# Expert weights of a mixture-of-experts layer: when they are loaded, in which order, and where their halves lie

## The reference

```
x = x + tanh(g_xattn) * xattn(layernorm(x), ctx, seg_id, Wq, Wkv, Wo)   # 16 heads, each token sees 4 context rows
x = x + tanh(g_ffn) * ffn(layernorm(x), gate_w, w1, b1, w2, b2)
# ffn: gate_probs = softmax(x @ gate_w.T); comb_w = the two largest probabilities, 0 elsewhere
for e in range(8):
    h = silu(x @ w1[e] + b1[e])            # w1[e]: 256 x 1024
    out = out + (h @ w2[e] + b2[e]) * comb_w[..., e]   # w2[e]: 1024 x 256
```

## Time and profile before

| | us |
|---|---|
| median of 3 runs (lowest, highest) | 345.33 (344.28, 345.51) |
| the profiled execution, device time | 344.77 |
| its span | 342.9 |
| PE busy | 312.0 (91%) |
| DVE busy | 250.8 (73%) |
| ACT busy | 189.5 (55%) |
| POOL busy | 198.6 (58%) |
| moved by DMA | 58.96 MB, 28.22 of them on q1 and 26.63 on q0 |

### The profile page before, as it was taken

The page is one execution under the profiler, slowest core; times in us unless marked ns, Lnnn a source line. Parts: engine busy times, 40 slices in busy tenths (PEclk is TensorE's granted clock), DMA queues, the critical chain, the costliest instruction groups (busy, mean ns, idle before and its releaser), DMA issues.

```text
span 342.9 us, 11216 instructions
## 1 busy us (share of the span) xinstructions
PE 312.0 (91%) x3305; PEld 253.4 (74%) x3305; DVE 250.8 (73%) x593; ACT 189.5 (55%) x526; POOL 198.6 (58%) x223
## 2 busy tenths in 40 slices
PE   7798989999998869999999999999999998999920
PEld 6457878888898658788878887878878776778710
DVE  4759999999998957868877688786886865464610
ACT  2451355665475358666767667667676655455410
POOL 2456889887764053346666666676676655663330
PEclk9899999999999999999999999999999999999985
DMA  7799999999899746245453553544545455453320
GB/s 249 235 341 417 403 419 404 414 405 387 292 381 383 259 105 161 39 76 77 67 95 56 89 88 60 93 66 79 85 68 86 79 66 95 54 94 45 35 22 10
DMA packets 51097, 58.96 MB, mean 172 GB/s; under 512 B 24424, under 2 KB 45120, under 8 KB 48864
## 3 DMA queue, kind: packets, MB, share of 16 engines
q0 software_dynamic: 9408, 26.63, 31.7%
q1 hardware_dynamic: 36320, 28.22, 26.8%
q10 hardware_dynamic: 5312, 3.37, 3.2%
HBM read 43.32 MB, written 10.16 MB: 156 GB/s over the span
## 4 chain that ended last, share of the span: by engine, by line
PE 64%; DVE 21%; issue 5%; ACT 3%; DMA 2%; POOL 2%; ACTq 0%; DVEq 0%; SPq 0%; POOLq 0%
PE ps L1143 29%; PE ps L1157 16%; PE ps L1158 8%; DVE ps L1312 5%; DVE sel L1308 2%; PE ps L1163 2%; DVE w_parts L1308 2%; PE ps L920 2%; DMA w_parts<-in_L_xattn_Wkv 2%; DVE xs L1344 1%; PE ps L1162 1%; PE ps L979 1%; DVE rden L1331 1%; DVE ps L1316 1%; PE ps L988 1%
## 5 line engine op out<-in xcount | busy, mean ns | idle before, releaser
L1143 PEld LDWEIGHTS ps<-sel,w_parts 128*128 x1776 | 120.9, 98 | 35.9 <-issue 4.0
L1143 PE MATMUL ps<-sel,w_parts 128*128 128x128 f16 x1776 | 142.1, 219 | 2.2 <-ACT sel L847 1.0
L627 POOL DMA_INDIRECT out<-sel x37 | 59.2, 1601 | 80.0 <-ACT sel L855 62.9
L869 ACT ACTIVATE sel<-ps,b1T 128x128 f32<-128x128 f32 x296 | 83.4, 368 | 29.7 <-PE ps L1143 26.2
L1157 PE MATMUL ps<-w_parts,sel 128*128 x259 | 96.0, 379 | 0.4 <-issue 0.3
L1158 PE MATMUL ps<-w_parts,sel 128*128 x259 | 70.6, 273 | 0.0
L1535 DVE SCALAR_TENSOR_TENSOR w_parts<-w_parts (+1 forms) x32 | 39.2, 1230 | 32.1 <-ACT w_parts L838 19.9
L619 POOL DMA_INDIRECT sel<-tokens_split,sel x37 | 45.1, 1219 | 16.9 <-DVE sel L1517 10.3
L1550 DVE SCALAR_TENSOR_TENSOR sel<-sel 128x512 f16<-128x512 f32 x74 | 51.2, 692 | 2.5
L1548 DVE TENSOR_SCALAR sel<-sel 128x512 f16<-128x512 f32 x74 | 31.9, 432 | 16.5 <-ACT sel L869 16.2
L855 ACT ACTIVATE sel<-xn,sel 128x256 f32<-128x256 f32 x37 | 18.8, 509 | 37.8 <-DVE xn L1590 34.1
(11 more groups left out here) (223 smaller groups left out, 423.2 us busy)
## 6 DMA issues: line engine op xcount, KB each, us to landing
w_parts<-in_L_ffn_w SPq DMA_DIRECT2D x16, 1024.0 KB
out<-xs SPq DMA_DIRECT2D x16, 128.0 KB
tokens_split<-xsplit ACTq DMA_DIRECT2D x13, 128.0 KB, 6.0
xs<-in_x ACTq DMA_DIRECT2D x2, 512.0 KB, 7.2
xs<-in_x SPq DMA_DIRECT2D x2, 512.0 KB, 6.9
near_rows<-w_parts SPq DMA_DIRECT2D x4, 256.0 KB, 6.2
xs<-in_L_ffn_b SPq DMA_DIRECT2D x1, 1024.0 KB
sel<-tokens_split,sel POOLq DMA_INDIRECT x37
```

Of the source, the lines that this page charges most:

```text
L627: pool.indirect_dma_start(out_rows, bass.IndirectOffsetOnAxis(slot_row[:, at(q - 1)], 0), y_sb[(k + 3) % 4], None, compute_op=ALU.add).the ...
L869: act.activation(h32[n][:, c * P:c * P + P], ps_h[n][:, c * P:c * P + P], ACT.Silu, bias=biases[:, c:c + 1], scale=1.0 / (X_SCALE * W_SCALE))\
L1143: mm = pe.matmul(ps_h[n][:, c * P:c * P + P], w, xx, start=(i == 0), stop=(i == len(products) - 1))
```

## The change

The expert weights are no longer loaded during attention. The ranks are sent through PE (a column of ranks), ACT, POOL (a one-hot matrix), PE (the expert of each rank) and ACT to POOL, which writes them as integers into `order_i`. SP then issues the first two weight DMAs (expert of rank 0) with a row offset from a register; two more come behind the DMA transpose of tile 1, and each further one behind the transpose of an even tile. Weight DMA t is now that of rank t//2. With that the splits have constant places: raw place u+2 to place u. ACT waits for each DMA by its own semaphore, in front of the split that reads it. PE reads one number for each tile, its rank, and none for tile 0. The computation of `tile_p` in the first steps and three DVE operations in front of the list (`order_i` from `r_rank`) are gone.

```diff
-        def weights_in(eng, t):
-
-            e, k = t // 2, t % 2
+        def weights_in(eng, e, t):
+
+            k = t % 2
             rows = (w1_rows, w2_rows)[k]
             n = (D, F)[k]
             dst = w_parts[:, 2 * t + 2:2 * t + 4, :, :].rearrange("p u a c -> p (u a c)").bitcast(F32)\
                 .rearrange("p (k n) -> p k n", k=n // P)
-            eng.dma_start(dst, rows[e * n:e * n + n, :].rearrange("(k p) n -> p k n", p=P)).then_inc(s[f"w_in{k}"], 16)
+            eng.dma_start(dst, rows[bass.ds(e * n, n), :].rearrange("(k p) n -> p k n", p=P)).then_inc(s[f"w_in{t}"], 16)
...
-                now, added = tiles_in(t, 0, -2)
-                if now and t % 2 == 0 and t < 14:
-                    sp.wait_ge(s["kprod"], t + 1)
-                    weights_in(sp, t // 2)
-                if t == T + 1:
-                    sp.wait_ge(s["aT_ps"], T)
-                    weights_in(sp, 10)
+                added, = tiles_in(t, -2)
                 if added:
                     sp.wait_ge(s["x1_ok"], t - 1)
                     sp.dma_start(out_v[t - 2], xs[:, t - 2, :]).then_inc(s["out_in"], 16)
-                if t == 13:
-                    for b in range(B):
-                        sp.wait_ge(s[f"kv_out{b}"], 16)
-                    sp.wait_ge(s["wT_ok"], 2)
-                    sp.wait_ge(s["sel_in7"], 32)
-                    for u in range(11, T):
-                        weights_in(sp, u)
-                if 14 <= t <= T:
-                    sp.wait_ge(s["aT_ps"], t - 1)
-                    weights_in(sp, t - 7)
...
             sp.dma_start(xd_comb[:, SEEN:T, :], r_comb[:, SEEN:T, :]).then_inc(s["comb_in"], 16)
+            for b in range(B):
+                sp.wait_ge(s[f"kv_out{b}"], 16)
+            sp.wait_ge(s["wT_ok"], 2)
+            sp.wait_ge(s["aT_ps"], T)
+            sp.wait_ge(s["order_ok"], 1)
+            ranked = [None] * E
+
+            def weights_of(t):
+
+                if t % 2 == 0:
+                    ranked[t // 2] = sp.value_load(order_i[0:1, t // 2:t // 2 + 1], min_val=0, max_val=E - 1)
+                weights_in(sp, ranked[t // 2], t)
+
+            weights_of(0)
+            weights_of(1)
...
             tokens_turned(1)
+            weights_of(2)
+            weights_of(3)
...
             for q in range(2, NT):
                 tokens_turned(q)
+                if q % 2 == 0 and q // 2 + 3 < 2 * E:
+                    weights_of(q // 2 + 3)
...
+            pool.wait_ge(s["rank_ok"], 1)
+            pool.tensor_scalar(rank_hot[:, :], iota[0:E, 0:E], rank_col[:, 0:1], None, ALU.is_equal).then_inc(s["rank_hot_ok"], 1)
+            pool.wait_ge(s["order_f_ok"], 1)
+            pool.tensor_copy(order_i[:, :], order_f[:, :]).then_inc(s["order_ok"], 1)
...
+            act.wait_ge(s["rank_ps"], 1)
+            act.activation(rank_col[:, :], ps_order[0:E, 0:1], ACT.Copy).then_inc(s["rank_ok"], 1)
             for e in range(E):
+                if e == E // 2:
+                    act.wait_ge(s["order_ps"], 1)
+                    act.activation(order_f[:, :], ps_order[:, E:2 * E], ACT.Copy).then_inc(s["order_f_ok"], 1)
...
+                    act.wait_ge(s[f"w_in{u // 2}"], 16)
                 wait(act, "w_lo_ok", u - 1)
-                act.activation(part(to, 0), place(raw), ACT.Copy, scale=W_SCALE).then_inc(s["w_hi_ok"], 1)
-
-            act.wait_ge(s["rt"], RT_ORDER)
-            for k in range(2):
-                act.wait_ge(s[f"w_in{k}"], 16 * E)
+                act.activation(part(u, 0), place(u + 2), ACT.Copy, scale=W_SCALE).then_inc(s["w_hi_ok"], 1)
...
-            spin(48)
+            spin(20)
+            pe.wait_ge(s["rt"], RT_RANK)
+            pe.matmul(ps_order[0:E, 0:1], r_rank[0:1, :], ident[0:1, 0:1], start=True, stop=True).then_inc(s["rank_ps"], 1)
+            spin(4)
+            pe.wait_ge(s["rank_hot_ok"], 1)
+            pe.matmul(ps_order[:, E:2 * E], e_row[:, :], rank_hot[:, :], start=True, stop=True).then_inc(s["order_ps"], 1)
...
-                        up_first = first_place[0] if q == -1 else block_byte(up, E)
+                        up_first = 0 if q == -1 else block_byte(up)
...
+                if q == -1:
+                    pe.wait_ge(s["rt"], RT_LIST)
+                    tiles.append(tile_count(pe))
...
-                raw, to = unit_places(dve, places, u)
                 dve.wait_ge(s["w_hi_ok"], u + 1)
-                v.scalar_tensor_tensor(out=part(to, 1), in0=place(raw), scalar=W_SCALE, in1=part(to, 0),
+                v.scalar_tensor_tensor(out=part(u, 1), in0=place(u + 2), scalar=W_SCALE, in1=part(u, 0),
```

More of the change, by code:

```diff
@@ L1119, in _, with block_byte @@
             spin(72)
-            pe.wait_ge(s["rt"], RT_LIST)
-            tiles = tile_count(pe)
-            before_of = [pe.alloc_register(f"before_{n}") for n in range(8 + NT - FULL - 4)]
-            expert_of = [pe.alloc_register(f"expert_{n}") for n in range(8 + NT - FULL - 4)]
+            tiles = []
+            rank_of = [pe.alloc_register(f"rank_{n}") for n in range(12)]
             w_bytes = w_parts[:, :, :, :].rearrange("p u a c -> p (u a c)").bitcast(U8)
-            def block_byte(register, top):
-                return pe.snap(pe.snap(register, min_val=0, max_val=top) * (4 * 2 * UC * 2))
+            def block_byte(register):
+                return pe.snap(pe.snap(register, min_val=0, max_val=E - 1) * (4 * 2 * UC * 2))
             def weights_at(first, unit, part, column, n):
@@ L1170, in first_tokens @@
                 mm.then_inc(s["xT_ps"], 1)
-            first_place = []
             def register(t):
-                return t % 8 if t < FULL + 4 else 8 + t - FULL - 4
+                return t % 8 if t < NT - 4 else 8 + t - (NT - 4)
             def registers_for(t):
-                n, some = register(t), slice(t, min(t + 4, NT))
-                count = some.stop - some.start
-                pe.reg_load(before_of[n:n + count], tile_p[0:1, some])
-                pe.reg_load(expert_of[n:n + count], tile_e[0:1, some])
+                n = register(t)
+                pe.reg_load(rank_of[n:n + 4], tile_r[0:1, t:t + 4])
             def moe(q, k, live):
@@ L1201, in moe @@
                     pe.wait_ge(s["w_lo_ok"], q + 3)
-                up, down = before_of[register(min(q + 1, NT - 1))], expert_of[register(max(q - 1, 0))]
+                up, down = rank_of[register(min(q + 1, NT - 1))], rank_of[register(max(q - 1, 0))]
                 if q + 1 >= FULL:
-                    with filled(pe, tiles, q - 1):
-                        first = block_byte(down, E - 1)
+                    with filled(pe, tiles[0], q - 1):
+                        first = block_byte(down)
                         pe.wait_ge(s["hlo_ok"], q * 2)
@@ L1211, in moe @@
                     if live(1):
-                        with filled(pe, tiles, q + 1):
-                            first = block_byte(up, E)
+                        with filled(pe, tiles[0], q + 1):
+                            first = block_byte(up)
                             turned(pe, q + 1)
@@ L1462, in _ @@
             v.memset(ps_list[:, 0:1], 0.0)
-            v.memset(tile_p[:, 0:4], 0)
             def count(ins):
@@ L1496, in _ @@
                                            op0=ALU.is_ge, op1=ALU.subtract).then_inc(s["tables"], 1)
-            ranks = iota[:, 0:E].rearrange("p (r o) -> p r o", o=1).to_broadcast([P, E, E])
-            link(v.tensor_tensor(r_by[:, :, :], spread_mid(r_rank[:, :], E), ranks, ALU.is_equal))
-            link(v.tensor_tensor(r_by[:, :, :], r_by[:, :, :], spread_mid(iota[:, 1:E + 1], E), ALU.mult))
-            with nc.allow_low_precision(reason="one small whole number and zeros"):
-                link(v.tensor_reduce(order_i[:, 1:E + 1], r_by[:, :, :], AX_X, ALU.add))
-            assert done[0] == RT_ORDER
             dve.wait_ge(s["tile_ok"], 1)
```

90 lines of the change are left out of this document (26 added, 64 removed).

## The result

| | before | after |
|---|---|---|
| median (lowest, highest), us | 345.38 (344.28, 345.51), 4 runs | 358.94 (355.64, 362.34), 4 runs |
| the profiled execution | 344.77 | 355.64 |
| its span | 342.9 | 353.8 |
| share of the DMA engines, 150 to 270 us | 0.48, 78 GB/s | 0.80, 168 GB/s |

The changed kernel is slower: ratio 1.0368, interval 1.0288 to 1.0448. Its profiled execution is the fastest of its four runs, so the traces show 10.9 us of a difference that is 13.6 in the medians.

What follows compares the result with a forecast made beforehand. It took DVE to bound attention and PE the expert stage; +4.3 + 1.5 - 0.55 - 0.3 = +4.95 on the profiled 344.77 gave 349.7, plus 0.56 made 350.2. Range 343.2 to 353.5, the forecast's own 347.5 to 352.

Steps and rivals of the forecast that it cites:

- Attention, nothing gained: Attention: relieving the DMA engines is worth nothing, since DVE waits for no transfer; its period stays 4.76 us.
- Routing, -0.35 and -1.2 + 0.4: Routing to tile 0: first product at 125.3 instead of 125.64; up product 1.2 us shorter, less 0.4 for moved register loads.
- The transpose of tile 2: Expert stage start: this transpose waits in q1 behind 3.15 MB, so PE starts tile 2 at 137.9, +4.3 us.
- The clock, +1.5: After PE's pause before tile 2: the clock falls to half rate, costing 1.5 us, between 0 and 2.
- "The steps after", -0.55 - 0.3: Expert steps: `tile_p` and its wait gone, -0.55 us; half of PE's register loads gone, -0.3 over the stage.
- "Hidden by some 0.9 us": Expert steps: with twelve later weight DMAs behind even transposes, odd transposes still land about 0.9 us before PE wants them.
- rival 3: Expert steps: odd transposes are late too, 0.5 us for each of twelve, adding 6 us: 356; chance 0.08.
- From the profile to the median: Whole kernel: 0.56 us added to the profiled execution's forecast, as the median before was that much higher.
- "weights hidden": Rival named only at tile 0's up product: 1.2 us higher by the skill page's gap; no chance given.
- rival 1: Tile 2: its transpose is not held up, no pause or clock loss, -1.95 us: 343.2; chance 0.20.

Runs made afterwards that it cites:

- e12_spun: Changed kernel with 100 products on a constant run on PE while it waits for the transpose of tile 2; 359.51 us.
- e4_index: Changed kernel with expert weights loaded during attention again, in index order, leaving out their sorting; 348.47 us.
- e5_index_al: e4_index with PE's four-word register loads all starting on a 16-byte boundary; 343.37 us.
- e6_before_off: Kernel before with its table of places moved by one word, so that its four-word register loads start off the 16-byte boundary; 351.11 us.
- e3_both: e1_early with PE's four-word register loads also aligned, except the last; 350.50 us.
- halves: e3_both with the last register load aligned and weight transfers from the third rank on cut in two, one half behind each transpose; 346.12 us.
- e1_early: Changed kernel with weight DMAs 2 and 3 issued ahead of tile 1's transpose, b2 behind tile 2's, later weights behind odd transposes; 354.29 us.

## Why the prediction was wrong

The direction was right, 350.2 was too low by 8.7 us, and 358.94 is outside the range. Of the 8.7, 1.0 arose up to the end of step 1, 5.1 in steps 2 to 30 and 2.7 between the profiled execution and the median. By its steps:

- **Attention, nothing gained**: right; the period is 4.76.
- **Routing, -0.35 and -1.2 + 0.4**: right, and a little better than said. The first gather started at 119.16 instead of 120.47, the first product of tile 0 at 124.26 where I had 125.3; counted from PE's first product of the routing (108.19, before 108.89) that is 0.7 earlier than before, for my 0.35. Tile 0 took 2.85. All of it ended in the pause and was worth nothing.
- **The transpose of tile 2**: right in mechanism and near in size. Tile 2 started at 138.60; I had 137.9, which is +5.0 for +4.3. The megabytes were through at 136.0, where I had 136.1. What was mis-sized is the transpose itself: its packets took 1.7 us (136.0 to 137.7), not 1.0, and it landed 0.9 behind them, not 0.7.
- **The clock, +1.5**: measured 1.9 (e12_spun). The sum's "up to 1.6" took the level to be back after 3.2 us; here it was low for 4.2 us of PE's work, 138.60 to about 142.8.
- **"The steps after", -0.55 - 0.3: this step failed.** In place of -0.85 stands +4.27. I counted register loads: half of PE's were gone, so the stage had to gain. Their duration I took over from before. The diff showed the new address (`tile_er`, 1860 + 39), and I did not read it. e4_index and e5_index_al put this alone at 5.9 us in the steps, 5.1 in the median; e6_before_off at 4.7 and 5.6.
- **"Hidden by some 0.9 us"**, the cover of the odd transposes: too thin, as rival 3 said, but it was priced as a wait behind one transfer on one ring. POOL's scatters land later too, on whatever queue the transfer is. With the loads aligned the profiled execution has 6.4 of excess (e3_both), of which halves take at least 4.3 away (4.9 less 0.6 for the last load). The two causes do not add up in the profiled executions: 5.86 (e4_index) and 6.41 (e3_both) alone, 8.48 together in e1_early, which differs from e3_both by the loads only, and 6.78 in after. A wait for a load and a late token can lie over each other; the excess of one execution is too uncertain to say by how much.
- **From the profile to the median** I added 0.56. The executions of after spread over 6.7 us, those of before beside them over 1.2 (2.7 to 4.4 in the 13 to 23 of later rounds), and the profiled one is the fastest of four: the median is 3.3 higher, and 2.7 of this are part of the miss. That this spread comes from DMAs which collide differently each time is a guess. The forecast took the 0.56 over from the kernel before, which has no weight transfers in its steps, and gave no reason for it.

Rival 3 (0.08; 356) came nearest in time, and this was in good part luck: late tokens do occur (e3_both shows them bare, 6.4 us for the 6 of the rival), but in the kernel after 5.35 of the 6.78 us lie in the steps behind the register loads, which the rival did not contain. The prediction also speaks of a rival "weights hidden"; none of its four has that name, and rival 1 is the nearest.

## What to carry to other kernels

When a table is moved or packed, check the address of every load of several registers from it as you would check an operand of a DMA: the count of loads says nothing if each takes three times as long. A transfer that is moved to a stretch with free bandwidth should come in pieces shorter than the slack of the small transfers beside it, on whatever queue, and its bytes must not stand in front of the first thing that PE needs. A loss that shares its steps with another can look small when it is removed alone (1.9 us for the alignment in the kernel after, 5.1 where no other loss was left): judge it in a kernel without the other.

## What the runs showed of the hardware

- PE's register load of four words takes 0.33 us (median) from an address that is a multiple of 16 bytes. From one word beside it, on either side, it takes 1.0 us at least (words 1899 and 1901), and from two words beside it as well (word 1934, the load of the kernel after at 182.7: 0.999). One of three words from a multiple of 16 bytes takes 0.77, four from there 0.33. The expectations split such a load into aligned pieces of four, two and one words; no run shows this, and the load at two words, which would be two pieces, speaks against it.
- Almost nothing hides such a load on PE: 0.67 us more for each made the seven steps behind them 4.5 us longer in e6_before_off (6.04 to 6.12 each, where before had 5.30 to 5.71).
- A transpose on q1 issued at 128.06 moved from 136.0 to 137.7, right behind the 3.1 MB issued before it and ahead of the megabyte issued 2.6 us after it.
- Transfers of 1 MB move POOL's scatters from 3.8 us between issue and landing (median) to 5.1 if they are on SP's queue and to 5.2 if they are on ACT's; transfers of 0.5 MB to 4.5.
